# Second routing of a two-layer MoE block: scatters issued back to back instead of one by one behind steps of the attention

## The reference, cut to what matters

```
x = x + 0.5 * ffn(layernorm(x))                 # 4096 tokens of 256, routed experts + a shared one
x = x + attention(layernorm(x))                 # 64-token segments, 8 heads, plus a global part
x = x + 0.5 * ffn(layernorm(x))                 # the same experts again

def ffn(x):
    scores = sigmoid(x @ gate.T)                # 32 experts in 8 groups
    # 4 best groups by score + bias, in them the 6 best experts; weights = scores / sum * 2.5
    # each expert: silu(x @ g.T) * (x @ u.T) @ down.T, summed over a token's six with its weights
    return routed + shared
```

## Time and profile before

| | |
|---|---|
| median of 3 runs | 1821.82 us (1819.31 to 1826.13) |
| the profiled execution | 1813.27 us, span 1811.4 us |
| TensorE busy | 1367.3 us (75%) |
| VectorE busy | 1035.4 us (57%) |
| ScalarE busy | 716.7 us (40%) |
| GpSimd busy | 897.4 us (50%) |
| second routing's scatters | 192, 196.3 us busy |

### The profile page before, as it was taken

The page is one execution under the profiler, slowest core; times in us unless marked ns, Lnnn a source line. Parts: engine busy times, 40 slices in busy tenths (PEclk is TensorE's granted clock), DMA queues, the critical chain, the costliest instruction groups (busy, mean ns, idle before and its releaser), DMA issues.

```text
span 1811.4 us, 47211 instructions
## 1 busy us (share of the span) xinstructions
PE 1367.3 (75%) x10480; PEld 1141.0 (63%) x10481; DVE 1035.4 (57%) x5308; ACT 716.7 (40%) x2232; POOL 897.4 (50%) x949
## 2 busy tenths in 40 slices
PE   6556655388888888879988888871878778787985
PEld 5445554377777777468666666641777777776664
DVE  6444553456556565557466666655555555555575
ACT  2222221155555555500455555430555555555300
POOL 4565556245444444422035555565345444444586
PEclk9666666599999999999888888855999999999998
DMA  9852223244444554387012222234444444544597
GB/s 321 293 198 94 98 101 111 82 149 148 142 149 148 161 164 148 108 298 260 8 64 102 102 98 98 103 114 158 136 138 152 142 145 139 181 146 130 180 303 249
DMA packets 154769, 274.52 MB, mean 152 GB/s; under 512 B 27942, under 2 KB 107067, under 8 KB 154688
## 3 DMA queue, kind: packets, MB, share of 16 engines
q1 hardware_dynamic: 116288, 160.27, 29.2%
q0 software_dynamic: 38400, 113.31, 16.9%
HBM read 146.59 MB, written 131.07 MB: 153 GB/s over the span
## 4 chain that ended last, share of the span: by engine, by line
PE 31%; issue 5%; DVE 4%; ACT 3%; DMA 3%; another core or an unknown queue 2%; POOL 1%; ACTq 1%; SPq 0%; DVEq 0%; POOLq 0%
PE ps L781 27%; DMA ans<-answers 3%; PE ps L904 3%; ACT xbt L1376 1%; ACT ans L1504 1%; POOL xres L763 1%; ACTq L1404 1%; PE ps L789 1%; DVE yb L2018 0%; PE ps L923 0%; DVE smax L2098 0%; DMA blk<-normed_transposed 0%; ACT xnt L1328 0%; DVE prob L2108 0%
## 5 line engine op out<-in xcount | busy, mean ns | idle before, releaser
L781 PE MATMUL ps<-xbt,ans 128*128 128x128 f32 x3072 | 422.7, 281 | 140.5 <-ACT xbt L1376 133.2
L781 PEld LDWEIGHTS ps<-xbt,ans 128*128 128x128 f32 x3072 | 380.5, 195 | 165.6 <-ACT ans L1386 122.2
L742 POOL DMA_INDIRECT answers<-yb,didx x208 | 204.5, 983 | 245.6 <-DVE yb L1896 180.1
L742 POOL DMA_INDIRECT answers<-ans,didx x208 | 204.4, 983 | 226.8 <-DVE ans L1896 152.5
L726 POOL DMA_INDIRECT dispatch_rows<-blk,idx x192 | 196.3, 1022 | 209.3 <-issue 116.7
L1886 DVE TENSOR_TENSOR hb<-ps,sg 128x128 f32<-128x128 f32 x416 | 120.6, 290 | 274.3 <-ACT sg L1396 176.7
L1386 ACT COPY ans<-wgu 128x512 f32 x416 | 255.6, 614 | 0.5 <-issue 0.5
L702 POOL DMA_INDIRECT dispatch_rows<-blk,idx x192 | 186.6, 972 | 139.4 <-issue 57.0
L1396 ACT ACTIVATE sg<-ps 128x128 f32<-128x128 f32 x416 | 115.8, 278 | 353.2 <-PE ps L781 306.4
L781 PE MATMUL ps<-wdn,hb 128*128 x768 | 232.3, 385 | 0.0
L1875 DVE SCALAR_TENSOR_TENSOR picked<-iota_e,etab,blk 128x32 f32<-128x32 f32 x832 | 177.0, 250 | 87.2 <-issue 34.2
(11 more groups left out here) (282 smaller groups left out, 2305.3 us busy)
## 6 DMA issues: line engine op xcount, KB each, us to landing
blk<-dispatch_rows SPq DMA_DIRECT2D x384, 160.0 KB
ans<-answers SPq DMA_DIRECT2D x54, 512.0 KB, 5.0
ans<-answers SPq DMA_DIRECT2D x54, 256.0 KB, 4.9
wgu<-in_gate_up SPq DMA_DIRECT2D x32, 256.0 KB
dispatch_rows<-blk,idx POOLq DMA_INDIRECT x384
dispatch_rows<-padt SPq DMA_DIRECT2D x32, 160.0 KB
blk<-dispatch_rows SPq DMA_DIRECT2D x64, 80.0 KB
yb<-answers SPq DMA_DIRECT2D x10, 512.0 KB, 4.8
```

The source lines that it names most:

```text
L742: pool.indirect_dma_start(out=answers_dram, out_offset=bass.IndirectOffsetOnAxis(ap=didx[:, q:q + 1], axis=0), in_=block_answers(q), in_of ...
L781: return nc.tensor.matmul(out_, lhs, rhs, start=start, stop=stop)
```

## The change

pool_route_paced is replaced by pool_route_free. A pair waits for its slots and its copied rows, as before, and its twelve scatters follow each other with no wait between them. All 16 pairs now run in one loop of 8 turns; before, 12 ran in a loop of 6 and 4 were written out. The scatters themselves, their order, their buffers and signals stay.

```
-                for t in range(2):
-                    i = p * 2 + (6 + t)
-                    for k in range(TOPK):
-                        if exists(i):
-                            event, value = step_of(i, k)
-                            if not isinstance(value, int) or value <= NT:
-                                pool.wait_ge(event, value)
-                                pool.sem_inc(s.take, 1)
-                        q = q0 + t
-                        pool.indirect_dma_start(...)
-            with pool.Fori(0, 6) as g:
+                for m in range(2 * TOPK):
+                    q, k = q0 + m // TOPK, m % TOPK
+                    pool.indirect_dma_start(
+                        out=rows_dram, out_offset=bass.IndirectOffsetOnAxis(ap=idx[:, q, k:k + 1], axis=0),
+                        in_=rows[:, q, :], in_offset=None).then_inc(s.scat[q], 16)
+            with pool.Fori(0, NT // 4) as g:
                 pair(g * 2, 0)
                 pair(g * 2 + 1, 2)
-            for p in range(12, NT // 2):
-                pair(p, 2 * (p % 2))
...
-            pool_route_paced(pool, R[1])
+            pool_route_free(pool, R[1])
```

More of the change, by code:

```diff
@@ L705, in pool_route_fours, with pool_route_free @@
             pairs_by_two(pool, lambda p, k: pair(p, 2 * k), NT // 2)
-        def pool_route_paced(pool, s):
-            def step_of(i, k):
-                return ((a_s, i + 1), (a_o, i), (a_qk, i + 3), (a_out, i), (a_v, i + 2), (a_pt, i + 1))[k]
+        def pool_route_free(pool, s):
             def pair(p, q0):
@@ L716, in pair @@
                 pool.sem_inc(s.take, 1)
-                for t in range(2):
-                    i = p * 2 + (6 + t)
-                    for k in range(TOPK):
-                        if exists(i):
-                            event, value = step_of(i, k)
-                            if not isinstance(value, int) or value <= NT:
-                                pool.wait_ge(event, value)
-                                pool.sem_inc(s.take, 1)
-                        q = q0 + t
-                        pool.indirect_dma_start(
-                            out=rows_dram, out_offset=bass.IndirectOffsetOnAxis(ap=idx[:, q, k:k + 1], axis=0),
-                            in_=rows[:, q, :], in_offset=None).then_inc(s.scat[q], 16)
-            with pool.Fori(0, 6) as g:
+                for m in range(2 * TOPK):
[4 more added lines that the diff above has]
+            with pool.Fori(0, NT // 4) as g:
                 pair(g * 2, 0)
                 pair(g * 2 + 1, 2)
-            for p in range(12, NT // 2):
-                pair(p, 2 * (p % 2))
         def pool_experts(pool, s):
```

## The result

The changed kernel takes 1913.02 us (median of 4 runs, 1903.22 to 1923.18) against 1820.57 us (4 runs, 1800.38 to 1826.13): the ratio is 1.0539, with a 95% interval of 1.0491 to 1.0587. It is slower by 92 us. Forecast were 1852 us and a range of 1817 to 1885; the direction was right and the size was not.

The account below looks back on a forecast made before the run. The attention was taken as bound by a chain of waits over TensorE, with scatter runs delaying signals. 13 pairs at +2.3 us gave +30 us, other terms 0: 1843 us profiled, 1852 us median, range 1817 to 1885.

Parts of the forecast that it names:

- The pair as the quantity: Attention with second routing: time per pair of tiles, 22.3 us with paced scatters, 3.8 us more than without.
- the 18.5 us of tiles 4 and 5: Attention pair with full routing but no scatter yet, taken as the time of a pair without loss.
- waits, buffers, loop and the stage's end: Second routing: removed waits, earlier free buffers and stage's end worth 0; loop 0.3 us only if its cover were gone.
- The mechanism: Attention: a long unbroken run of scatters delays signals between engines, more so the longer it is.
- the two marks that would have proved it wrong: Attention pairs still at 22.3 us (run length not the cause), or below 21.5 us (waits or places the cost).
- the loss of a run of twelve is 6.1 us: Attention pairs 0 to 12: each becomes one run, taking 24.6 us, 2.3 us more; times 13 pairs, +30 us.
- The two places: Long runs in the trace before: attention's end, 6.8 us scaled to twelve, and first routing, 5.5 us; middle 6.1 us.
- the run of thirteen: End of the attention stage, 1208.86 to 1225.12 us: delays of 7.4 us in all, 6.8 us scaled to twelve.
- the run of sixteen: First routing: VectorE waits some 9.6 us on its own results between 160.4 and 170; upper bound +75 us.
- Rival (c): Attention: nearly no progress during a run, as in the first routing; +75 us, 1897 us; chance 0.07.
- Rival (a): Attention: only the port GpSimd shares with VectorE counts, and stays hidden; 1822 us, at most 3 us more; chance 0.23.
- Rival (b): Attention: scatters' place counts, not run length; mix gaps and low-clock stretches saved, -15 us, 1807 us; chance 0.10.

Follow-up runs that it names:

- no_scatter: The changed kernel with four small-tile clears by GpSimd in place of each second-routing scatter; 1850.49 us against 1848.12 us for the kernel before.
- short_twos: The changed kernel with a 1.1 us pause (one clear) after every second scatter of a pair; 1845.59 us against 1839.06 us before, ratio 1.0032.

## Why the prediction was right in direction and wrong in size

*The pair as the quantity, right; its base, wrong.* All of the added time lies in the pairs. But the 18.5 us of tiles 4 and 5 are not what a later pair takes without a loss: that stretch has 259 matmuls and a later pair 226 (1808 in eight), on a chip without standstills it takes 18.5 us as well, and the later pairs there take 16.6 under the same scatters; in no_scatter they take 16.2 to 17.7. Against 16.6 us the paced scatters cost 5.7 us a pair, not 3.8, and a run of twelve 13.7. The difference between the kernels, 8.0 us, doesn't depend on the base.

*No gain and no price from waits, buffers, loop and the stage's end, right.* From the second table to the end both kernels take 548.2 us, and where there are no standstills the whole change is worth 0.2% or nothing.

*The mechanism, right in its cause.* Twelve scatters 1.27 us apart in every pair, late signals in the run and none behind it; they come from the fourth scatter on, not in the second half alone, and ScalarE's longest wait marked "remote" in the pair shown is 7.85 us (at 1046.94), not 2 to 5. Neither of the two marks that would have proved it wrong came (pairs at 22.3 us, or below 21.5).

*The term that failed: "the loss of a run of twelve is 6.1 us".* On the forecast's own base it is some 12 us: 30.3 - 18.5 = 11.8. The pairs were to be 24 to 26 us apart and are 30.3, the pauses 8 to 10 us and are 15.5. 13 pairs times 8.0 us in place of 2.3 are 104 us in place of 30; the profiled difference in the stage is 98. The two places were read on the wrong engines. I added up how late ScalarE's copies and VectorE's own chain were. But in the run of thirteen TensorE's lines have these two waits, behind its mix at 1209.39:

```profile
1215.66 2.07 PE L781 MATMUL ps<-wol,ans 128*128 128x256 f32 x4 [5.58 <-issue]
1224.04 0.66 PE L789 MATMUL ps<-ident,yb 128*128 128x128 f32 x2 [3.74 <-issue]
```

They are 9.3 us for thirteen scatters; and in the run of twelve of the first routing it waits again for "issue" 0.91, 1.74 and 1.16 us, the first of them during VectorE's 4.54. "issue" there doesn't mean that the engine had nothing to do. The size was there to be seen in the run of sixteen, where TensorE stands 13.22 us before this line; in most other places of that routing the same wait is 0.46 to 0.66 us:

```profile
173.79 1.06 PE L781 MATMUL ps<-wgate,xnt 128*128 128x32 f32 x4 [13.22 <-ACT xnt L1328]
```

Of the same run VectorE's five waits between 160.4 and 170 were given as 9.6 us; they add up to 8.5, and the rest is its work. The forecast also treated a run as a fixed delay of some signals, where in the attention it is a standstill that grows with the run: it begins at about the fourth scatter and ends some 2 us after the last. Rival (c), "nearly no progress during a run", had the mechanism and 1897 us; it was given 0.07 though the run of sixteen that spoke for it was the only one with much work left to hold up.

*Rival (a), the shared port*, is out as the whole price: a scatter beside VectorE's products is longer (1.07 at 1033.78 here), but in the first 4.5 to 5 us of the standstill VectorE stands like the others (4.76 us before 1038.76), so no instruction of VectorE is there to contend with, and a GpSimd busy with clears costs no such time. *Rival (b), place*: the mixes behind the run are undisturbed, as it said, but the mean granted clock fell instead of rising (0.73 against 0.84), with TensorE idle 11.1 us a pair in place of 3.7.

*What none of the cases had*: that the loss is there on some chips and not on others. The forecast and the timing agree in sign only for chips like the one of the profile; on chips of the other kind the same change is worth nothing.

*Open.* What in a scatter stops the others (GpSimd's making of descriptors, the number of rows, the completion signals), and why three chips don't have it, or whether it is the chips at all; whether it is the run or a backlog behind it; whether the place of a run in the pair matters; whether runs of two with no joined run would beat the kernel before on a chip with standstills. None of the runs is a version that beats both kernels: the best of them on such a chip, short_twos, is level with the kernel before (1.0032, 0.9994 to 1.0071). The chips may also differ in more than shows in these traces.

## What to carry to other kernels

Where TensorE waits for "issue" or a signal is "remote" beside a stream of GpSimd's indirect DMAs, add up the busy time of every engine across the run, not the late signals of one, and compare the length of the same work with and without the stream. Pace such a stream by events of the work beside it: fixed pauses cost 5% where they were not needed, the waits for the attention's steps cost nothing there and save 5% where they are. And a stage whose length differs between chips by a quarter, while its neighbour without scatters doesn't, is a warning that a tuning result may hold for that kind of chip alone.

## What the runs showed of the hardware

- On some chips a run of GpSimd's indirect DMAs stops the other engines. In the attention with runs of twelve the first three leave them alone, and from about the fourth on they nearly stand until some 2 us after the last (eleven of thirteen pairs; in the first routing TensorE works through nine of sixteen first). The pause of 1.1 us in short_twos did not end the standstill of 1077.7 us; runs of four cost 24.8 us a pair with pauses of 2.3 us and 28.5 with 1.1.
- It is the same with 256 bytes a row as with 1280 (30.6 and 30.3 us a pair), and the DMA engines are busy 21% in the stage. An indirect DMA keeps GpSimd 0.97 us either way. That agrees with the Trainium skill, "Perfetto Trace Analysis", section "DMA Instruction — SWDGE (GPSIMD)": the end that the profile records is the end of making the descriptors, not of moving the data.
- On three other chips 180 and more such DMAs stand 1.28 us apart without a break in the first routing, and no wait is "remote" in any of the ten traces. The same kernel then takes 1477 in place of 1820 to 1848 us.
- Beside its idle time TensorE pays by the clock: the same 1808 matmuls keep it busy 153.3 us at a mean granted clock of 0.73 with standstills and 122.4 us at 0.96 without.
